# Diffusion attention: the products with v taken two chunks at a time, every eighth step, with the probabilities in three buffers

## The reference, cut to what matters

```python
qk = (x @ Wqk).reshape(b, n, H, dh).transpose(0, 2, 1, 3)
v = (x @ Wv).reshape(b, n, H, dh).transpose(0, 2, 1, 3)
dot = jnp.einsum('bhnd,bhmd->bhnm', qk, qk)
q2 = jnp.sum(qk * qk, axis=-1)
logits = (2.0 * dot - q2[..., :, None] - q2[..., None, :]) / math.sqrt(dh)
attn = jax.nn.softmax(logits * tau, axis=-1)
out = jnp.einsum('bhnm,bhmd->bhnd', attn, v)
```

## Time and profile before

| | |
|---|---|
| runs, median | 4227.38 us |
| profiled execution, its own time | 4227.27 us |
| its span in the profile | 4225.5 us |
| mean granted TensorE clock | 0.931 of full |
| diffusion attention in the span | about 2783 to 3642 us |
| TensorE busy, whole span | 3640.5 us (86%) |
| VectorE, ScalarE, GpSimd busy | 57%, 41%, 37% |

### The profile page before, as it was taken

How to read it: one execution, slowest core, us unless ns; L and a number is a source line. 1 busy time by engine, 2 the same in 40 slices (tenths; PEclk the granted TensorE clock), 3 DMA queues, 4 the chain that set the end, 5 groups by cost and what they waited for, 6 DMA issues and landing times. The chain is left out here.

```text
span 4225.5 us, 59934 instructions
## 1 busy us (share of the span) xinstructions
PE 3640.5 (86%) x17328; PEld 2176.8 (52%) x17328; DVE 2420.3 (57%) x6561; ACT 1748.9 (41%) x3994; POOL 1582.0 (37%) x1718
## 2 busy tenths in 40 slices
PE   6999999999689998998999989769999999569940
PEld 3556655556445555554555556434555554446620
DVE  6676776767466663234565523436666665455557
ACT  2544554445345554112555521125555555124410
POOL 2343433433367664002766622421222221442244
PEclk8999999999799999999999999969999999679975
DMA  6565765557201102453010122222222221269942
GB/s 104 69 80 66 94 86 82 77 62 91 59 31 50 50 35 70 164 202 119 26 50 35 38 74 70 62 72 63 57 57 67 57 57 44 104 199 319 317 152 70
DMA packets 230321, 377.77 MB, mean 89 GB/s; under 512 B 39822, under 2 KB 166098, under 8 KB 223698
## 3 DMA queue, kind: packets, MB, share of 16 engines
q1 hardware_dynamic: 218770, 356.77, 35.6%
q0 software_dynamic: 6144, 16.79, 1.2%
q10 hardware_dynamic: 5184, 1.58, 0.2%
HBM read 170.03 MB, written 84.93 MB: 60 GB/s over the span
## 5 line engine op out<-in xcount | busy, mean ns | idle before, releaser
L758 DVE CUSTOM_DVE_ANT_0 a_ps<-a_ps,a_mask 128x128 f32<-128x128 f32 (+3 forms) x1024 | 479.9, 512 | 194.1 <-PE a_ps L513 176.3
L2479 ACT ACTIVATE c_probsT<-c_ps 128x512 f32<-128x512 f32 x512 | 298.6, 600 | 335.4 <-PE c_ps L2301 326.2
L368 POOL TENSOR_SCALAR_AFFINE_SELECT a_probs_c<-a_probs_c 128x256 f32<-128x256 f32 (+1 forms) x384 | 187.4, 504 | 664.6 <-ACT a_probs_c L663 664.4
L2618 DVE TENSOR_REDUCE c_neg_max<-c_ps 128x1 f32<-128x512 f32 x512 | 337.1, 684 | 160.4 <-PE c_ps L2289 159.0
L663 ACT ACTIVATE a_probs_c<-a_ps 128x512 f32<-128x512 f32 x640 | 344.9, 603 | 100.0 <-PE a_ps L531 75.0
L513 PE MATMUL a_ps<-a_packed_qk 65*128 65x128 f32 (+3 forms) x1024 | 338.3, 374 | 47.3 <-DVE a_maxima L758 26.8
L1094 POOL TENSOR_TENSOR w_probs<-w_probs,w_inv 128x1024 f32<-128x1024 f32 x128 | 242.3, 1893 | 334.8 <-DVE w_inv L1457 334.8
L549 PE MATMUL a_ps<-a_probs_c,a_v 128*64 128x512 f32 (+3 forms) x2048 | 316.6, 453 | 1.0 <-POOL a_probs_c L368 0.8
L531 PE MATMUL a_ps<-a_packed_qk 67*128 67x512 f32 (+3 forms) x1024 | 288.5, 344 | 1.6 <-DMA a_packed_qk<-a_max_half 1.5
L2289 PE MATMUL c_ps<-c_packed_qk 68*128 68x512 f32 x512 | 256.1, 506 | 10.5 <-DVE c_neg_max L2618 6.6
L1349 ACT ACTIVATE w_probs<-w_ps_s,w_neg_max 128x256 f32<-128x256 f32 x512 | 235.9, 478 | 66.9 <-DVE w_neg_max L1452 66.2
(11 more groups left out here) (323 smaller groups left out, 7723.5 us busy)
## 6 DMA issues: line engine op xcount, KB each, us to landing
a_packed_qk<-a_halves SPq DMA_DIRECT2D x512, 128.0 KB, 4.6
d_w<-in_L_ffn_second SPq DMA_DIRECT2D x71, 516.0 KB, 4.9
d_w<-in_L_ffn_first SPq DMA_DIRECT2D x71, 512.0 KB, 5.0
rows_dram<-f_zeros SPq DMA_DIRECT2D x8, 4096.0 KB, 15.7
c_packed_qk<-c_halves SPq DMA_DIRECT2D x256, 128.0 KB, 2.3
w_v<-w_v_next SPq DMA_DIRECT2D x16, 1024.0 KB, 4.6
d_rows<-rows_dram SPq DMA_DIRECT2D x71, 128.0 KB, 4.2
mixed_dram<-d_y SPq DMA_DIRECT2D x71, 128.0 KB, 4.8
```

The source lines that it names most:

```text
L758: last = nc.vector.tensor_tensor_reduce(tile, tile, mask[:, (NT - 1 - i) * P:], 1.0, -3e38, ALU.add, ALU.max, accum_out=maxima_of[:, hd // ...
L2479: nc.scalar.activation(probsT[:, q % 2, r, :], ps_again[u % 2][:, :], ACT.Exp).then_inc(exp_done.sem, 1)
L2618: nc.vector.tensor_reduce(neg_max[:, g % 2, 0, s % GS:s % GS + 1], bank("s", s)[:, :], AX.X, ALU.max, negate=True).then_inc(max_ready.sem, 1)
```

## The change

The chunks 2k and 2k + 1 are multiplied one behind the other in step 8k + 7 (counted with the lag); no chunk is multiplied in steps 3, 11, 19, 27, 35, 43, 51, 59. The probabilities get three parts in place of two, and chunk q uses part `SET[q % 4]`: even chunks alternate between parts 0 and 2, odd chunks share part 1. The waits for a part to be free and for the exponentials follow.

```diff
+    SET = (0, 1, 2, 1)
...
-        probsT = sb("probsT", [P, 2, HG, N])
+        probsT = sb("probsT", [P, 3, HG, N])
...
-                pe.wait_ge(exp_done.sem, exp_done.at(b, HG * (q + 1)))
+                if q % 2 == 0:
+                    pe.wait_ge(exp_done.sem, exp_done.at(b, HG * (q + 2)))
...
-                    last = nc.tensor.matmul(ps_o[ROWS * r:ROWS * (r + 1), :], v[:, c, HG * g + r, :], probsT[:, q % 2, r, :],
+                    last = nc.tensor.matmul(ps_o[ROWS * r:ROWS * (r + 1), :], v[:, c, HG * g + r, :], probsT[:, SET[q % 4], r, :],
...
-                if s % HG == 3:
+                if s % (2 * HG) == 7:
                     d, q = (0, (s - LAG - 2) // HG) if s >= LAG + 2 else (-1, (s - LAG - 2 + STEPS) // HG)
                     if d in live:
+                        weigh(ref(b, d), q - 1, d - 1 in live)
                         weigh(ref(b, d), q, d - 1 in live)
...
                 if r == 0:
-                    if q >= 2:
-                        act.wait_ge(pv_done.sem, pv_done.at(b, q - 1))
+                    back = 2 if q % 2 else 4
+                    if q >= back:
+                        act.wait_ge(pv_done.sem, pv_done.at(b, q - back + 1))
                     elif prior:
-                        act.wait_ge(pv_done.sem, pv_done.at(ref(b, -1), CHUNKS + q - 1))
-                nc.scalar.activation(probsT[:, q % 2, r, :], ps_again[u % 2][:, :], ACT.Exp).then_inc(exp_done.sem, 1)
+                        act.wait_ge(pv_done.sem, pv_done.at(ref(b, -1), CHUNKS + q - back + 1))
+                nc.scalar.activation(probsT[:, SET[q % 4], r, :], ps_again[u % 2][:, :], ACT.Exp).then_inc(exp_done.sem, 1)
```

## The result

The changed kernel takes 4336.76 us (median of 4 runs, 4323.51 to 4343.15) against 4228.47 us for the kernel before: ratio 1.0255, 95% interval 1.0223 to 1.0287. It is slower, as forecast, but by 108 us where 33 were forecast, and it lies outside the range of 4230 to 4280.

The account below looks back on a forecast made before the run. Chains through ScalarE, VectorE or a DMA, not TensorE's busy time, were taken to hold up nearly every half batch. 28.1 (full batches) + 3.0 (batch 7) + 1.5 (drain) = +32.6 on 4227.3 gave 4260 us, range 4230 to 4280.

Parts of the forecast that it names:

- Second chunk: On TensorE, the second chunk of each pair costs 0.90 us, bounded by 0.86 and 1.00.
- Rival D: The second chunk's weight loads are not hidden: 0.87 us more a pair, +56, so 4316 us; chance 0.03.
- Steps 3, 11, 19, 35, 43: Lone chunks removed here lie inside hold-ups by ScalarE, VectorE or a DMA; removing each gives back 0.
- Step 27: After the removed chunk, TensorE can turn the outputs once VectorE has them ready: 0.59 us back.
- Steps 51 and 59: Removing these lone chunks gives back 0.99 us in step 51 and 0.94 in step 59.
- Sum of a full batch at full clock: 8 x 0.90 less 2.52 given back: +4.68 us a full batch, 28.1 for batches 1 to 6.
- Batch 7 and the drain: Batch 7, without a next batch's work, costs +3.0 us; the drain's pairs cost +1.5 us, estimated.
- The clock: Falls to half clock, 3.1 us each in three of six full batches, in steps 11 to 12; left unchanged in the sum.
- rival C: The clock falls in every full batch after longer idle in steps 7 and 11: +9.3, 4269 us; chance 0.12.
- its own signs: Expected in the profile: step 7's wait over 1 us, three VectorE waits about 1 us longer, a wait before step 22's L2301.
- Rival A: TensorE is the bound, the hold-ups only apparent; each removed chunk returns 1.18 us: -18, so 4209 us; chance 0.08.
- Rival B: Half of the pairs' extra time meets unseen slack in steps 3 to 47's real waits: 4227 to 4243 us; chance 0.17.

Follow-up runs that it names:

- e8: The changed kernel with the scores matmul issued again, output unchanged, in steps where TensorE waits (6, 7, 11, 12, 20 and others): 4276.99 us.
- e4: The changed kernel with the products of all even chunks left out and the exponentials scaled by 0.001, so the output differs: 4265.32 us.
- e9: Against the kernel before: odd chunks of steps 31, 47, 63 delayed four steps to join even chunks of 35, 51, 3, three parts kept: 4220.53 us.
- e2: The changed kernel with only the pairs of steps 7 and 39, all other chunks alone as before, three parts kept: 4261.95 us.

## Why the prediction was wrong, point by point

**Direction and mechanism: right.** Five of the eight chunks taken away did lie inside hold-ups, and the pair's second chunk is paid in full. Where the clock holds, the changed schedule can be read term by term. The starts are taken from TensorE's timeline, in us from the batch's turned maxima in step 0 (3086.85 before, 3102.10 in e8). The growth is that of the shift since the row above; where TensorE gets nothing back it is the pair's 0.86:

| step | before, lone chunk | e8, pair | shift | growth |
|---|---|---|---|---|
| 7 | 7.55 | 7.45 | -0.10 | |
| 15 | 19.70 | 20.44 | 0.74 | 0.84 |
| 23 | 27.01 | 28.57 | 1.56 | 0.82 |
| 31 | 40.47 | 43.21 | 2.74 | 1.18 |
| 39 | 52.08 | 55.68 | 3.60 | 0.86 |
| 47 | 69.09 | 73.53 | 4.44 | 0.84 |
| 55 | 85.22 | 89.35 | 4.13 | -0.31 |
| 63 | 94.33 | 98.49 | 4.16 | 0.03 |
| next batch | 95.99 | 101.01 | 5.02 | 0.86 |

**Second chunk.** Forecast 0.90 between 0.86 and 1.00; measured 0.86. Rival D (weight loads not hidden, 0.87 more a pair) is out: sixteen instructions take 1.85 us. The row of packed products was the better guide than the rule of the Trainium skill ("TensorE: Matmul & The Clock Gate", its part on packing small matmuls), which in the same place also lets a load go ahead of running matmuls when it goes to the background weight buffer, a case that the forecast left out.

**Steps 3, 11, 19, 35, 43: nothing given back.** Behind steps 11, 19, 35 and 43 the growth is 0.82 to 0.86, so 0.00 to 0.04 came back, and step 3 gave back 0.10 (the first row). Right, five times, to within 0.10. I assigned the reason by one end time within 0.1 us of one start each, and that was enough.

**Step 27.** Forecast 0.59 back. In the batch of the changed kernel that begins at 3122.80 the pair of step 23 ran at full clock, and the shift grows by 0.72 from step 23 to step 31, so 0.14 came back (in e8 two fills of 0.235 are added). One line of the kernel before, then three of that batch:

```profile
3118.40 0.60 PE L2328 MATMUL c_ps<-ident,c_sumsT 128*128 128x128 f32 x4
```
```profile
3161.33 0.60 PE L2331 MATMUL c_ps<-ident,c_sumsT 128*128 128x128 f32 x4
...
3162.83 0.63 PE L2256 MATMUL c_ps<-ident,c_o 128*128 128x128 f32 x4 [0.44 <-DVE c_o L2646]
...
3165.54 1.97 PE L2339 MATMUL c_ps<-c_wo,c_oT 128*128 128x256 f32 x8 [0.34 <-ACT c_oT L2506]
```

The turned outputs start 1.50 us behind the turned sums, where it was 1.99 before (3118.40 to 3120.39), so 0.49 came back there. Then TensorE waits 0.34 for ScalarE's copy of the turned outputs, a wait that I had not followed.

**Steps 51 and 59.** Forecast 0.99 and 0.94 back, measured 0.86 + 0.31 = 1.17 and 0.83. e4 has 1.18 and 0.83 for the removals alone. In step 51 the removal gives back the full 1.18, of which I had counted only the distance behind the chunk.

**Sum of a full batch at full clock.** Forecast +4.68 (4.4 with 0.86), measured +5.0 in e8, fills included. Six batches: 28.1 against 30.

**Batch 7 and the drain.** Forecast +3.0 and +1.5, measured +13 and +7 at clocks of 0.92 and 0.76. Part of it is the clock again: 0.92 over 100.4 us is 16 us at half speed, worth up to 8, where before there was none. So some 5 of the 13 at least are not the clock, more than the 3.0 of the forecast; I didn't separate the rest.

**The clock: the step that failed.** I wrote "Three more falls would add 9.3 us, three fewer take 9.3 away. I leave the number as it is in the sum", and gave rival C 4269 us. The sum took the clock at nothing, and rival C named the mechanism at a quarter of its price. I had counted falls as one place (step 11) that either has one or hasn't. In the changed kernel two full batches fall in steps 7, 12, 39 and 44, and the other four in four or five places, one of them just ahead of or at the pair of step 23. The mean clock of 0.91 over 108.9 us is 20 us at half speed in each batch, against none or 6.8 before, and it costs 7.9 us a batch (108.9 - 101.0), 47 us in the six; the kernel before had lost 9 of these already, so 38 are new, against 9.3 in rival C. The forecast listed the grown waits in its own signs ("over 1 us" in step 7, "about 1 us each" in three more places, a new wait in step 22) and did not carry them over to the clock, step by step.

**Rival A** (TensorE is the bound, 4209) is out: it wanted more than 0.90 back from a removed chunk on average, and in e8, at full clock, 8 x 0.86 - 5.02 = 1.86 us come back from eight, 0.23 each. That e4 isn't faster does not exclude it alone, because its clock fell too. **Rival B** (partly absorbed) is out: the full batches lose 30 us at full clock, no less than the forecast had.

The account in the span: 30 us for the schedule in six batches, 38 for the clock there (68 - 30), 24 in batch 0, batch 7 and the drain, 12 in blocks that did not change, 104 in all. The forecast had 28, nothing, 4.5 and nothing for these four, so the clock in the full batches is the largest part that it missed.

What stays open: how much of the 24 us in batch 0, batch 7 and the drain is schedule, whether the 12 us in the other blocks have to do with the change, and how many falls the kernel before has in a typical run.

## What to carry to other kernels

A chunk of work that fills an engine's wait is free, and moving it to a place where the engine isn't held up costs its time (e9 moves chunks the other way and gains a little): read what ends just before the next instruction, not the busy share. On TensorE such work had a second use here, it kept the granted clock up, so when an edit widens waits, list each widened wait and price a stretch of half clock behind each one. Two experiments settle such a case quickly: the removal without the addition, and repeated matmuls in the waits; if a version that computes more is faster, at a higher granted clock, it was the clock.

## What the runs showed of the hardware that I had not expected

Leaving out half of the products made the kernel 36 us slower (e4: 4265 against 4230), with TensorE's clock in the full batches at 0.91 in place of 0.98. The same program falls in one batch and not in the next with identical work: 97.66 us at 1.00 is followed by 103.36 us at 0.93 in e2. Four column-tiled matmuls of 512 columns, two instructions each, take 1.00 us to the next matmul alone and 0.86 more as the second of a pair.
